# Attention pooling on one core: the chunks in their own layout loaded from ScalarE's queue, the transposed ones from SyncE's

## What is computed

```python
h = relu(einsum('bse,eh->bsh', behavior_emb, W_b) + (candidate_emb @ W_c)[:, None, :] + fc1_b)
scores = einsum('bsh,h->bs', h, fc2_w[:, 0]) + fc2_b[0]
attn = softmax(scores, axis=-1)
user_interest = einsum('bse,bs->be', behavior_emb, attn)
x = concatenate([user_interest, candidate_emb], axis=1)
logit = (relu(x @ mlp1_w + mlp1_b) @ mlp2_w + mlp2_b)[:, 0]
```

## Time and profile before

| | |
|---|---|
| median of 3 runs | 266.75 us |
| the profiled execution's own time | 266.47 us |
| its span in the profile | 264.7 us |
| TensorE, matmuls busy | 259.3 us (98%) |
| VectorE busy | 224.2 us (85%) |
| ScalarE busy | 200.6 us (76%) |
| GpSimd busy | 29.4 us (11%) |
| read from HBM | 105.63 MB |
| share of the chain that ended last: TensorE, DMA, VectorE | 60%, 18%, 14% |

### The profile page before, as it was taken

One profiled execution on the slowest core, in us unless ns is written; L12 is line 12 of the kernel. 1 busy time (PEld: TensorE's weight loads), 2 busy tenths in 40 slices (PEclk: granted clock), 3 DMA queues, 4 the chain that ended last, 5 costly groups with the idle time before them and its releaser, 6 DMA issues.

```text
span 264.7 us, 10384 instructions
## 1 busy us (share of the span) xinstructions
PE 259.3 (98%) x3942; PEld 212.4 (80%) x3942; DVE 224.2 (85%) x397; ACT 200.6 (76%) x481; POOL 29.4 (11%) x38
## 2 busy tenths in 40 slices
PE   8999999999999999999999999999999999999995
PEld 7557788888888868888888888888888888888973
DVE  0479998999898988989899998989989898999541
ACT  2569888798887697878789887878888787889312
POOL 2003001111110111110111111011111100111100
PEclk9999999999999999999999999999999999999999
DMA  7999999999999999999999999999999999999900
GB/s 247 430 433 422 422 426 420 424 424 420 426 422 423 426 420 429 429 426 426 424 429 429 426 426 426 428 428 422 428 429 428 426 426 426 429 428 426 391 32 0
DMA packets 10544, 105.87 MB, mean 400 GB/s; under 512 B 1184, under 2 KB 1696, under 8 KB 2592
## 3 DMA queue, kind: packets, MB, share of 16 engines
q1 hardware_dynamic: 10240, 105.44, 94.7%
q10 hardware_dynamic: 288, 0.20, 0.2%
HBM read 105.63 MB, written 0.00 MB: 399 GB/s over the span
## 4 chain that ended last, share of the span: by engine, by line
PE 60%; DMA 18%; DVE 14%; issue 4%; ACT 1%; DVEq 1%; POOL 0%; ACTq 0%; SPq 0%; POOLq 0%
DMA xt<-in_behavior_t 18%; PE s_ps L632 12%; PE u_ps L643 11%; PE z_ps L617 10%; PE z_ps L613 9%; DVE xl L454 9%; PE z_ps L614 8%; DVE hidden L464 5%; PE z_ps L608 4%; PE z_ps L750 2%; PE z_ps L643 1%; ACT xh L329 1%; PE z_ps L684 1%; PE z_ps L727 1%; PE z_ps L721 1%
## 5 line engine op out<-in xcount | busy, mean ns | idle before, releaser
L454 DVE TENSOR_TENSOR xl<-xt,xh 128x800 fp32r<-128x800 f32 x120 | 123.2, 1047 | 8.9 <-ACT xh L329 8.7
L329 ACT CAST xh<-xt 128x800 fp32r<-128x800 f32 x120 | 100.4, 862 | 34.2 <-DMA xt<-in_behavior_t 33.1
L371 ACT ACTIVATE hidden<-z_ps,bias 128x200 f32<-128x200 f32 x256 | 88.3, 428 | 7.4 <-PE z_ps L608 3.6
L613 PE MATMUL z_ps<-xh,w_hi 128*128 128x512 f32 x240 | 86.4, 360 | 0.5 <-DVE hidden L464 0.5
L614 PE MATMUL z_ps<-xh,w_lo 128*128 128x512 f32 x240 | 79.4, 345 | 0.0
L464 DVE TENSOR_TENSOR hidden<-z_ps,neg_bias 128x800 f32<-128x800 f32 x64 | 62.9, 982 | 3.3 <-PE z_ps L608 2.0
L617 PE MATMUL z_ps<-xl,w_hi 128*128 128x512 f32 x240 | 64.8, 351 | 0.9 <-DVE xl L454 0.2
L613 PEld LDWEIGHTS z_ps<-xh,w_hi 128*128 128x128 f32 x240 | 45.0, 188 | 16.3 <-issue 6.0
L299 POOL TENSOR_TENSOR weights_by_row<-weights,masks_sb 128x400 f32<-128x400 f32 x31 | 27.6, 890 | 218.3 <-ACT weights L336 177.3
L632 PE MATMUL s_ps<-hidden,f_col 128*3 128x160 f32 (+4 forms) x1280 | 50.1, 301 | 0.0
L614 PEld LDWEIGHTS z_ps<-xh,w_lo 128*128 128x128 f32 x240 | 45.1, 188 | 5.6
(11 more groups left out here) (65 smaller groups left out, 77.6 us busy)
## 6 DMA issues: line engine op xcount, KB each, us to landing
x<-in_behavior SPq DMA_DIRECT2D x32, 1600.0 KB, 26.6
xt<-in_behavior_t SPq DMA_DIRECT2D x30, 1600.0 KB, 23.7
xt<-in_behavior_t SPq DMA_DIRECT2D x4, 400.0 KB, 4.9
xt<-in_behavior_t SPq DMA_DIRECT2D x2, 800.0 KB, 7.7
later_sb<-in_later SPq DMA_DIRECT2D x1, 258.5 KB, 19.6
first_sb<-in_cand_rest SPq DMA_DIRECT2D x1, 192.0 KB, 5.7
first_sb<-in_first ACTq DMA_DIRECT2D x1, 128.0 KB, 4.8
masks_sb<-in_masks SPq DMA_DIRECT2D x1, 114.0 KB, 6.8
```

Source lines behind the costliest of these rows:

```text
L329: nc.scalar.copy(xh[g][:, :], xt[q][:, g, :]).then_inc(xh_made, 1)
L371: op = nc.scalar.activation(hidden[q % 2][:, g, :, mine], z[:, :, mine], ACT.Relu, bias=bias[:, bass.ds(c * ROWS + g * EACH + b, 1)])
L454: nc.vector.tensor_tensor(xl[g][:, :], xt[q][:, g, :], xh[g][:, :].bitcast(F32), ALU.subtract).then_inc(xl_made, 1)
L613: nc.tensor.matmul(z[:, a:b], w_hi[:, :], xh[g][:, a:b], start=True, stop=False)
```

## The change

The loads of `x` leave SyncE's queue. ScalarE's sequencer now issues them, between the relu of group 3 (in period 1, the cast that follows it) and the last `xh` of the period. In period 1 it issues x0, in period 2 x1 and x2, in period 3 x3 and x4, and from then on in period c the load of chunk c+1, behind a wait for the weighted sum of chunk c-3. SyncE issues the `xt` loads alone, by the same waits as before, and `later_sb` moves from behind x0 to behind xt31.

```diff
@@ -251,29 +251,15 @@
                     sp.wait_ge(xl_made, (c - XT_BUFS + 1 - WHOLE) * GROUPS)
                 sp.dma_start(xt[buf][:, :, :], behavior_t[c, :, :, :]).then_inc(xt_loaded[buf], 16)
 
-            def load(c, buf):
-
-                if buf is None:
-                    buf = c
-                else:
-                    sp.wait_ge(pooled_done, c + (1 - X_BUFS))
-                sp.dma_start(x[buf][:, :], behavior_v[c, :, :]).then_inc(x_loaded[buf], 16)
-
 
             for c in range(2, X_BUFS):
                 load_transposed(c, None)
-            load(0, None)
-            sp.dma_start(later_sb[:, :], later).then_inc(later_loaded, 16)
             for c in range(X_BUFS, 2 * X_BUFS):
                 load_transposed(c, c - X_BUFS)
-                load(c - LAG, None if c - LAG < X_BUFS else c - LAG - X_BUFS)
             with sp.Fori(0, CHUNKS // X_BUFS - 2) as turn:
                 for j in range(X_BUFS):
-                    c = turn * X_BUFS + (2 * X_BUFS + j)
-                    load_transposed(c, j)
-                    load(c - LAG, (j - LAG) % X_BUFS)
-            for c in range(CHUNKS - LAG, CHUNKS):
-                load(c, c % X_BUFS)
+                    load_transposed(turn * X_BUFS + (2 * X_BUFS + j), j)
+            sp.dma_start(later_sb[:, :], later).then_inc(later_loaded, 16)
             for part, (a, b) in enumerate(PART_CHUNKS):
                 sp.wait_ge(logit_made, part + 1)
                 sp.dma_start(out[a * ROWS:b * ROWS].rearrange("(g n) -> g n", g=GROUPS),
@@ -327,6 +313,12 @@
                     act.wait_ge(z_done, c * GROUPS + (g + 1 - GROUPS))
 
                 nc.scalar.copy(xh[g][:, :], xt[q][:, g, :]).then_inc(xh_made, 1)
+
+            def load(c, buf, early):
+                if not early:
+
+                    act.wait_ge(pooled_done, c + (1 - X_BUFS))
+                act.dma_start(x[buf][:, :], behavior_v[c, :, :]).then_inc(x_loaded[buf], 16)
 
             def exponents(c, buf, early):
                 act.wait_ge(softmax_step, c * SOFTMAX_STEPS + SOFTMAX_STEPS)
@@ -409,6 +401,11 @@
                     exponents(c - 1, (q + 1) % 2, phase <= 2)
                     next_half(2)
                     biased_relu(c, q, 3, phase)
+
+                for n in {1: [0], 2: [1, 2], 3: [3]}.get(phase, []):
+                    load(n, n, True)
+                if LAG <= phase < LAST:
+                    load(c + 1, nq, False)
                 next_half(3)
 
             periods(period)(act)
```

## The result

The changed kernel takes 269.67 us (269.21 to 270.19), the kernel before, measured beside it, 266.64 us. The ratio is 1.0118, with a 95% interval of 1.0099 to 1.0137: 3.0 us slower, where 1.2 us was forecast. Of the 3.0 us, 2.6 lie inside the span; the rest lies outside it (2.1 us around the instructions in place of 1.8).

A forecast was written before the change was run, and what follows sets the result against it. The prediction took xt's arrival on full DMA engines as the bound. x landing 4.1 us later, less 2.7 us margin, gave TensorE's tail +1.3, less 0.1 won back: +1.2 us, 267.9 us, range 265.6 to 270.3.

The forecast's parts named there:

- What bounds the kernel before: Whole loop: arrival of xt sets the pace, 7.69 us a period; x has 2.74 and 2.41 us of margin.
- turn: Prediction's unit: the time the DMA takes for one chunk in one layout, 1.638 MB, 3.85 us.
- The rate of two queues: DMA throughout: two queues move bytes at the rate of one, term 0, bounded by 2.3 us either way.
- Equal shares: While both queues have work, with equal 12.8 KB packets, each gets half and the lead is kept.
- ScalarE's part: ScalarE's x issues, 0.41 to 0.47 us each, run beside the relu and cost nothing.
- Rivals B: ScalarE's issues: 0.44 us uncovered in each period makes the kernel slower, +7.8 us, 274.5 us; chance 0.04.
- A's early issue: Period 1: sequencer comes to x0's issue at 16.4 us, lead 3.5 turns, x only 1.2 us later.
- The lead: Turns of xt ahead of x when x0 starts to move, at 20.2 us: 4.26, with x landing 4.1 us later.
- rival S: Follow-up experiments' rival: the lost time comes from ScalarE's issues and waits, wherever they stand; 3 us, no chance given.
- xt and the end: xt 1.0 us earlier, 1.7 with later_sb; at the end x28 to x31 land as before, 0.1 us comes back.
- Rival A: Start of x: x0 goes out early, lead below 3.9 turns, faster, 265.6 us; chance 0.22 with the rate's gain.
- Rival C: Period 1: sequencer lets the cast end at 21.3, x0 moves at 22.3, +3.3 us, 270.1 us; chance 0.09.

The follow-up runs named there:

- e6: Kernel before, one queue, with only later_sb moved from behind x0 to behind xt31; 265.91 us, ratio 0.9974.
- e7: Kernel before, one queue, no x load on ScalarE, each x load one xt load later in SyncE's queue; 268.09 us, ratio 1.0055.
- e1: Changed kernel, x0 issued 4.7 us earlier, behind the group 1 relu of period 1, and x1 where x0 was; 268.54 us, ratio 1.0080.
- e2: Changed kernel, x0 issued 2.6 us earlier, behind the first xh of period 1, and x1 where x0 was; 267.75 us, ratio 1.0044.
- e3: Changed kernel, x0 issued later, in period 2 together with x1 and x2; 272.84 us, ratio 1.0247.
- e5: Changed kernel, with later_sb back ahead of xt4 in SyncE's queue; 269.68 us, ratio 1.0118.
- e8: Changed kernel, xt3 and xt4 each loaded as four one-group loads with 3.2 KB rows; 268.00 us, ratio 1.0050.
- e4: Changed kernel, x0 alone issued by SyncE behind xt3, x1 to x31 still by ScalarE; 267.82 us, ratio 1.0045.
- e9: Kernel before, one queue, later_sb behind xt31, x loads in column halves, the second half one xt load later; 269.79 us, ratio 1.0127.
- e11: Kernel before, one queue, later_sb not moved, xt and x loaded in alternating halves from chunk 4 on; 273.32 us, ratio 1.0259.
- e10: Kernel before, plus three 16 KB loads from ScalarE's queue into a tile that nothing reads; 266.81 us, one run.
- e12: As e9, but x cut by partitions, 0 to 63 and 64 to 127, with whole 12.8 KB rows; 475.44 us.

## Why the prediction was off

- **What bounds the kernel before.** Right. `xt` sets the pace and `x` has 2.4 to 2.7 us of margin: e6 gained the 0.7 us by moving `later_sb`, and e7 lost 1.5 us by one turn of `x`.
- **The rate of two queues.** Right: 426 GB/s in both. The Trainium skill, "DMA: Bandwidth & Descriptors", section "Issuing engines are not separate DMA queues", has loads of several issuing engines run on the same 16 DMA engines; by it there was no bandwidth to win, and the 426 GB/s of both traces agree.
- **Equal shares.** Right. The bytes by queue of the kernel after between 60 and 230 us (packets, MB, share of the 16 engines):

```profile
q10 hardware_dynamic: 3179, 36.14, 50.3%
q1 hardware_dynamic: 3177, 36.16, 50.3%
```

- **ScalarE's part.** Right: the issues run beside the relu, at 18.98 for the 19.2 that was forecast. Rivals B and A's early issue are out by this row.
- **The lead.** The step that failed is "the DMA engines begin at 1.7 [...], 1.0 us later. So x0 starts to move at 20.2". The 1.0 us was taken from idle engines at the start of the kernel and used in the middle of a stream, where it is 3.6. With the issue at 18.98, x0 moves at 22.56, 2.4 us later than forecast. By the same sum the lead is 4.26+2.4/3.85 = 4.88 (the bytes of the queues give 4.7), and `x` lands 4.1+2.4 = 6.5 us later. In the first periods it does: x7, issued at 59.84 and 26.6 us on its way, lands at 86.44, where in the kernel before it was issued at 53.85, took 26.1 and landed at 79.95.
- **What reached the end.** x26 lands 232.38-227.13 = 5.25 us later. The rest is that the kernel before loses 1.3 us between x7 and x8 (79.95 to 88.92, where 7.7 is usual), and the changed kernel does not (86.44 to 94.17). 5.25 less the margin of 2.74 and with the 0.13 between landing and start is the 2.64 us by which the weighted sum is late. This was luck: without the step, whose cause no run shows, `x` would have stayed 6.5 us late, and the kernel would have been about 1.3 us slower still.
- **Outside the span.** The prediction put ScalarE's issues at nothing, and inside the span that held. But 2.1 to 2.2 us lie around the instructions in every execution of the changed kernel and of e1, e2, e3, e5 and e8, 1.9 in e4, and 1.8 in every kernel that loads no `x` from ScalarE (the one before, e6, e7, e9, e11). This 0.3 us is a small share of rival S; it does not depend on the lead, and what it consists of is open.
- **xt and the end.** Right: xt31 was to land at 237.0 and landed at 237.05, and the last `x` near 254 and landed at 254.5. Compute gave back nearly nothing.
- **Rival A.** Its price was wrong too. It has a lead of 3.5 with `xt` still early and the kernel faster, 265.6. e1 has this lead and took 268.54: by the prediction's own count `xt` is late from 3.8 turns down.
- **Rival C** named this size, by another way (a late issue instead of a late start). It had x0 moving at 22.3 and it moved at 22.56, but its condition, an issue at 21.3, was wrong; that its price, 3.3 us, is about right is luck.

The mechanism was as forecast, `x` late and TensorE stopped before the weighted sums. One term, the time from x0's issue to its first bytes, was 1.0 us in the sum and 3.6 in the run; two smaller ones, the step and the time outside the span, were not in it.

## What to carry to other kernels

Where the DMA is the limit, the order of a single queue is a schedule: each transfer has the full rate and lands as early as its place allows. Two queues that share give each transfer half the rate, so both land at the end of both, and the phase between them is set by whatever happened when the second one started. In this kernel the best of the phases tried was still 0.4% slower than one queue. So before loads are split over queues, ask how much slack each of them has, and take latencies for a new queue from a moment when the engines are as busy as they will be.

## What the runs showed of the hardware

- A load on the second queue starts 3.4 to 3.6 us after its issue while the other queue keeps the DMA engines full (first packet of x0 in the changed kernel, e1, e2, e3, e5 and e8, of x1 in e4, and of the small loads in e10), and about 1 us when they are idle (start of the kernel, e10's last load). A load of 16 KB took 9.1 to 9.4 us beside a stream of 12.8 KB rows and 1.6 us alone.
- The same bytes moved at 426 GB/s with all rows at 12.8 KB, at 422 with `x` in halves, at 418 with both in halves, and at 235 with `x` in loads of 64 partitions (e12).
- After an idle stretch of TensorE that began at 29.2 us, the granted clock was 0.50 from 35 to 41 us, and 56 weighted-sum matmuls took 2.90 us in place of 1.58 (e3).
- In the kernel before all landings step back by 1.3 us once, near 88 us; in the changed kernel `x` does not (`xt` does, by 1.5 us between xt12 and xt13). An instruction fetch falls about there, as eight did before it. What makes this one count is open; no run was made for it.
